# A recommendation tower on one core: unrolled h copied to PSUM, one split remainder made by GpSimd, and ten of layer 1's sixteen tiles split

## The reference, cut to what matters

```python
e = jnp.stack([tbl_0[ids[:, 0]], ..., tbl_31[ids[:, 31]]], axis=1)     # x: 1024 x 32 fields x 32
def _cin(x, Ws, bs):
    h = x
    for i, (W, b) in enumerate(zip(Ws, bs)):                            # O = 128, 128, 1
        z = jnp.einsum('bhd,bmd,ohm->bod', h, x, W.reshape(O, H, F))
        z = jax.nn.relu(z + b[None, :, None])
        if i < n_layers - 1:
            h, direct = (z[:, :half, :], z[:, half:, :])                # 64 rows go on, 64 are summed
        ...
    return jnp.sum(jnp.concatenate(directs, axis=1), axis=-1)
z = _cin(e, (W0, W1, W2), (b0, b1, b2))
h = relu(concat([z, dense_ctx]) @ W_top1 + b_top1); h = relu(h @ W_top2 + b_top2); y = h @ W_top3
```

## Time and profile before

| | us |
|---|---|
| time, median of 3 runs | 1158.95 (1157.48 to 1160.01) |
| span of the profiled execution | 1162.5 |
| busy: PE / DVE / ACT / POOL | 1116.8 / 1083.0 / 458.8 / 520.5 |
| first matmul | 28.4 |

### The profile page before, as it was taken

How to read it: one execution, slowest core, us unless ns; L and a number is a source line. 1 busy time by engine, 2 the same in 40 slices (tenths; PEclk the granted TensorE clock), 3 DMA queues, 4 the chain that set the end, 5 groups by cost and what they waited for, 6 DMA issues and landing times.

```text
span 1162.5 us, 10957 instructions
## 1 busy us (share of the span) xinstructions
PE 1116.8 (96%) x3608; PEld 652.8 (56%) x3608; DVE 1083.0 (93%) x604; ACT 458.8 (39%) x383; POOL 520.5 (45%) x270
## 2 busy tenths in 40 slices
PE   0699999999999999999999999999999999999998
PEld 0355555556555555556555565555555555555554
DVE  1599999999999999999999999999999999999963
ACT  0134444333444433344444334444333444443424
POOL 6702445654445555454456544455555544450000
PEclk9899999999999999999999999999999999999999
DMA  7654543466554435555543455454445545433200
GB/s 222 200 165 129 148 136 118 108 153 162 161 139 137 126 108 143 161 161 139 132 135 106 140 161 161 139 146 128 112 129 160 161 140 160 131 123 96 55 1 0
DMA packets 63413, 154.94 MB, mean 133 GB/s; under 512 B 12753, under 2 KB 29394, under 8 KB 63394
## 3 DMA queue, kind: packets, MB, share of 16 engines
q1 hardware_dynamic: 52562, 146.98, 42.5%
q0 software_dynamic: 8192, 4.21, 3.0%
q10 hardware_dynamic: 2640, 3.50, 1.0%
HBM read 95.79 MB, written 8.39 MB: 90 GB/s over the span
## 4 chain that ended last, share of the span: by engine, by line
PE 93%; issue 2%; DVE 2%; ACTq 1%; another core or an unknown queue 1%; ACT 1%; DMA 0%; SPq 0%; DVEq 0%
PE z_ps L543 89%; PE u_ps L543 2%; PE mlp_ps L543 1%; DVE raw L450 1%; DVE prod_lo L457 1%; DVE prod L411 1%; DMA h_roll<-h_roll 0%; SPq L328 0%; ACT prod_hi L760 0%; SPq L329 0%; ACT h_roll L729 0%; ACT direct L747 0%; ACTq L713 0%; ACTq L715 0%
## 5 line engine op out<-in xcount | busy, mean ns | idle before, releaser
L543 PE MATMUL z_ps<-prod,w_sb 128*128 128x512 f32 x1536 | 692.8, 597 | 39.2 <-issue 28.4
L303 POOL DMA_INDIRECT gathered<-in_table,rows_sb x256 | 504.9, 1972 | 499.5 <-DVE h2x L464 428.8
L543 PEld LDWEIGHTS z_ps<-prod,w_sb 128*128 128x128 f32 x1536 | 292.7, 191 | 350.6 <-issue 333.8
L760 ACT CAST prod_hi<-raw 128x2048 fp32r<-128x2048 f32 x128 | 243.9, 1905 | 396.5 <-DVE raw L450 389.4
L450 DVE TENSOR_TENSOR raw<-h_roll,x_roll 128x2048 f32<-128x2048 f32 x128 | 293.1, 2290 | 5.6 <-DMA h_roll<-h_roll 2.1
L457 DVE TENSOR_TENSOR prod_lo<-raw,prod_hi 128x2048 fp32r<-128x2048 f32 x128 | 292.0, 2281 | 2.6 <-ACT prod_hi L760 2.6
L411 DVE TENSOR_TENSOR prod<-h_roll,x_roll 128x2048 f32<-128x2048 f32 x128 | 292.6, 2286 | 0.0
L543 PE MATMUL z_ps<-prod_hi,w_hi 128*128 128x512 f32 x520 | 215.4, 494 | 0.4 <-DVE prod_lo L457 0.4
L543 PE MATMUL z_ps<-prod_lo,w_hi 128*128 128x512 f32 x520 | 164.1, 395 | 0.0
L543 PE MATMUL z_ps<-prod_hi,w_lo 128*128 128x512 f32 x520 | 163.8, 395 | 0.0
L411 DVE TENSOR_TENSOR prod<-x_base,x_roll 128x2048 f32<-128x2048 f32 x63 | 143.4, 2286 | 12.8 <-DMA x_roll<-x_dram 10.8
(11 more groups left out here) (56 smaller groups left out, 240.8 us busy)
## 6 DMA issues: line engine op xcount, KB each, us to landing
x_roll<-x_dram SPq DMA_DIRECT2D x128, 512.0 KB
x_base<-x_dram SPq DMA_DIRECT2D x32, 512.0 KB
h_roll<-h_roll SPq DMA_DIRECT2D x32, 448.0 KB, 4.6
h_roll<-h_roll SPq DMA_DIRECT2D x32, 384.0 KB, 5.4
h_roll<-h_roll SPq DMA_DIRECT2D x32, 320.0 KB
x_dram<-gathered SPq DMA_DIRECT2D x64, 128.0 KB
h_roll<-h_roll SPq DMA_DIRECT2D x32, 192.0 KB
gathered<-in_table,rows_sb POOLq DMA_INDIRECT x256
```

What stands on the lines that cost most here:

```text
L303: nc.gpsimd.indirect_dma_start(gathered[:, u, g * DIM:(g + 1) * DIM], None, table, bass.IndirectOffsetOnAxis(ap=rows_sb[:, col:col + 1], a ...
L543: return nc.tensor.matmul(*args, **kw)
L760: nc.scalar.copy(prod_hi[:, b % SPLIT_RING, :, :], raw[:, :, :]).then_inc(hi_ready, 1)
```

## The change

Layer 1's sixteen tiles are shared out anew: three whole pairs and five split pairs. The whole pairs are (a=1; x 0, 1), (a=0; x 0, 1) and (a=0; x 2, 3); the split pairs are B0 to B3 (a = 2, 3 by x 0, 1, 2, 3) and A1 (a=1; x 2, 3).

- ScalarE copies the unrolled h (a=0) into the PSUM tile `mlp_ps`, which only the last network used (`copy_h0`, one copy of 128 x 1024 a chunk). The two whole pairs with it read h from PSUM and x from SBUF.
- The remainder of B1 is made by GpSimd (`lo1`), the other four by VectorE.
- The gathers are issued a chunk at a time, three chunks ahead, each after the `lo1` of its step; before, they went out in groups of four chunks.
- Buffers: `prod` has two pairs (three before), `raw` two (one), `prod_hi` and `prod_lo` three (two), `x_base` one (two), and `top_b` is `x_base`, zeroed in the last chunk by GpSimd.
- The loads of `x_roll` 0 and 1 wait for the first two whole products of layer 1 two chunks before, 2 and 3 for B2 and B3; `x_part16` is loaded between.
- `sum_direct` and `layer2` come after the two products from PSUM.

```diff
-PAIRS1 = ROLLS
-RING = 3
-SPLIT_RING = 2
+WHOLE1 = 3
+B0, B1, A1, B2, B3 = range(5)
+SPLIT1 = 5
+RING = 2
+SPLIT_SLOT = (0, 1, 2, 0, 1)
+SPLIT_RING = 3
+RAW_SLOT = (0, 1, 0, 1, 0)
...
+            def lo1(c):
+                rounded = settled(pool, c * SPLIT1 + B1 + 1)
+                behind = settled(pool, lo_count(c, B0))
+                pool.wait_ge(hi_ready, rounded)
+                pool.wait_ge(lo_ready, behind)
+                nc.gpsimd.tensor_tensor(prod_lo[:, SPLIT_SLOT[B1], :, :], raw[:, RAW_SLOT[B1], :, :],
+                                        prod_hi[:, SPLIT_SLOT[B1], :, :], ALU.subtract).then_inc(lo1_ready, 1)
...
+                    base_free = settled(sp, first0(c - 1) + PAIRS0)
+                    free = [(prod_ready, settled(sp, first1(c - 2) + 2))] * 2 + [
+                        (raw_ready, settled(sp, (c - 2) * SPLIT1 + r + 1)) for r in (B2, B3)]
...
+                if isinstance(c, int) and c == 1:
+                    sp.wait_ge(prod_ready, PAIRS0)
+                    load_base(c)
...
-                for b in range(ROLLS):
-                    whole(first1(c) + b, slot1(c) + b, h_roll[:, s, 0:PAIR, :], twice(x_roll[:, s, b, :]))
+                split_product(c, u, B0)
+                if not is_last(c):
+                    split_rest16(c + 1)
+                if not is_first(c):
+                    rolled_once()
+                split_product(c, u, B1)
+                split_rest(c, B0)
+                dve.wait_ge(h0_copied, c + 1)
+                for k in range(PAIRS0):
+                    whole(first1(c) + 1 + k, slot1(c, u) + 1 + k, twice(mlp_ps[:, :]),
+                          x_roll[:, s, k * PAIR:(k + 1) * PAIR, :])
+                if not_first(c):
+                    layer2(c - 1, *before)
+                    sum_direct(c - 1, *before)
+                split_product(c, u, A1)
+                split_product(c, u, B2)
+                split_rest(c, A1)
+                split_product(c, u, B3)
+                split_rest(c, B2)
...
+                layer1(c, u, 0)
+                if not is_last(c):
+                    layer0_pairs16(c + 1)
+                if not_first(c):
+                    layer2_u(c - 1, (u - 1) % UNROLL)
+                split(z1_ps, c, B0)
+                layer1(c, u, 1)
+                split(z1_ps, c, B1)
+                layer1(c, u, 2)
+                split(z1_ps, c, A1)
+                split(z1_ps, c, B2)
...
+            def copy_h0(c, u):
+                act.wait_ge(h1_ready, 2 * (c + 1))
+                if not_first(c):
+                    act.wait_ge(prod_ready, first1(c - 1) + WHOLE1)
+                nc.scalar.copy(mlp_ps[:, :], h_roll[:, u % 2, 0, :]).then_inc(h0_copied, 1)
```

More of the change, by code:

```diff
@@ L96, in y_partition, with pool_makes_lo3, lo_count @@
     return FIELDS * j
-assert (PAIRS0 + PAIRS1) % RING == 0 and PAIRS1 % SPLIT_RING == 0
+def pool_makes_lo3(c):
+    return False
+def lo_count(c, r):
+    if not isinstance(c, int):
+        return c * LO_PER_CHUNK + LO_ORDER[r]
+    return sum(LO_PER_CHUNK + (0 if pool_makes_lo3(k) else LO_EXTRA) for k in range(c)) + LO_ORDER[r]
+assert UNROLL % RING == 0
 def build_tower(nc, gather_ids, row_base, table, w0, w0_swapped, w1_whole, w1_split, w2, b0, b1, b2,
@@ L282, in _, with make_rows @@
             pool.wait_ge(ids_loaded, 32)
-            def gather_group(group):
+            def make_rows(group):
                 cols = UNROLL * GATHERS
-                made = settled(pool, group + 1)
-                freed = [0 if isinstance(group, int) else settled(pool, (group - 1) * UNROLL + u + 1)
-                         for u in range(UNROLL)]
                 for u in range(UNROLL):
@@ L293, in gather_group, with gather @@
                                         ALU.add).then_inc(rows_made, 1)
+            def gather(c, u, group):
+                made = settled(pool, group + 1)
+                freed = settled(pool, c - UNROLL + 1)
                 pool.wait_ge(ids_loaded, 32)
                 pool.wait_ge(rows_made, made)
[L297 to L306, removed]
@@ L308, in _ @@
-            gather_group(0)
-            with pool.Fori(1, CHUNKS // UNROLL) as group:
-                gather_group(group)
+                wait(pool, h2x_ready, freed)
+                for g in range(GATHERS):
+                    col = u * GATHERS + g
+                    nc.gpsimd.indirect_dma_start(
+                        gathered[:, u, g * DIM:(g + 1) * DIM], None, table,
+                        bass.IndirectOffsetOnAxis(ap=rows_sb[:, col:col + 1], axis=0),
+                    ).then_inc(gather_done[u], 16)
@@ L312, in _ @@
+            make_rows(0)
+            for c in range(UNROLL - 1):
+                gather(c, c, 0)
+            over_chunks(pool, step)
         @block.sync
@@ L427, in products0 @@
                         dve.wait_ge(x_roll_loaded[s][b], (c - s + 2) * 8)
-                    whole(first0(c) + k, slot0(c) + k, twice(x_base[:, s, :]), x_roll[:, s, k * PAIR:(k + 1) * PAIR, :])
+                    whole(first0(c) + k, slot0(c, u) + k, twice(x_base[:, :]), x_roll[:, s, k * PAIR:(k + 1) * PAIR, :])
                 dve.wait_ge(gather_done[u], (group + 1) * (16 * GATHERS))
@@ new lines, in rolled_once @@
+                def rolled_once():
+                    dve.wait_ge(h1_ready, 2 * (c + 1))
+                    dve.wait_ge(h1_rolled[s][0], (c - s + 2) * 16)
+                    whole(first1(c), slot1(c, u), twice(h_roll[:, s, 1, :]), x_roll[:, s, 0:PAIR, :])
+                if is_first(c):
+                    rolled_once()
[3 more added lines that the diff above has]
+                if not is_first(c):
+                    rolled_once()
@@ L865, in lay_out @@
     w1 = a["L0_rec_W1"].reshape(P, HID, FIELDS)
[L866 removed]
+    whole = [(1, 0), (1, 1), (0, 0), (0, 1), (0, 2), (0, 3)]
+    split = [(2, 0), (3, 0), (2, 1), (3, 1), (1, 2), (1, 3), (2, 2), (3, 2), (2, 3), (3, 3)]
+    for name, tiles in (("w1_whole", whole), ("w1_split", split)):
         arrays[name] = np.stack([w1[:, (r + H_ROLL * k) % HID, (i + x_shift(quad, b)) % FIELDS].T
[L868 removed]
+                                 for k, b in tiles], axis=1)
     w2 = a["L0_rec_W2"].reshape(HID, FIELDS)
```

219 lines of the change are left out of this document (121 added, 98 removed).

## The result

The change made the kernel slower: 1166.81 us, median of five runs (1165.20 to 1170.21), beside 1160.01 for the kernel before on the same chip (1157.48 to 1161.79). The ratio is 1.0062 with a 95% interval of 1.0046 to 1.0077, so the loss of 0.6% is small but clear of the noise. The forecast was 1140.

A forecast was written before the change was run, and what follows sets the result against it. TensorE was taken as the bound at 33.80 us a chunk, VectorE only 0.37 faster. Gains of 17.7 over 30 chunks, 1.3 at the start and 0.6 at the end made 19.6: 1158.95 to 1139.4, called 1140 for scatter; range 1134 to 1157.

The forecast's parts named there:

- what covers GpSimd's remainder: Layer 1: GpSimd's estimated 4.6 us run from 8.2 to 12.8, hidden beside VectorE's PSUM products, 1.2 us to spare before A1.
- the ring of two: VectorE in layer 1: earliest held at the last whole product, at 10.1 us after TensorE's start on layer 0.
- 1.0 us later: Layer 1's first whole pair needs `relu1` by 6.7, gets it at 5.6; VectorE may run up to 1.0 us late.
- Rival C: VectorE and TensorE wait in turn through ScalarE, losing 0.5 to 0.6 us a chunk: 1157 to 1161; no-change chance 0.05.
- TensorE's need: TensorE per chunk: one split pair replaces a whole one, -0.63 us, from 33.80 to 33.17.
- products from PSUM at no extra cost: VectorE's layer 1 products reading h from PSUM: assumed to cost no more than from SBUF, nothing taken.
- rival B: PSUM products are held by GpSimd too, 4.0 us more a chunk: 1287, or 1213; chance 0.13, shared with long GpSimd overrun.
- VectorE's list: VectorE per chunk: fourteen large instructions still, two fewer waits of 0.11, so from 33.43 to 33.21 us.
- Rival A: GpSimd's subtraction overruns its window, costing from 5.8 us: 1150 at 6.1, over 1159 beyond 6.4; small-loss chance 0.14, shared.
- The start: First chunks: TensorE's start on chunk 2 counts as 85.0 against 86.29, a gain of 1.3 us.
- The bridge: Span to median: median taken as 3.55 us below the span, so span 1142.9 gives 1139.4.
- 0.6 at the end: Last chunk, bound by TensorE again: a gain of 0.6 us.

The follow-up runs named there:

- Experiments 1: Kernel after the change, with ScalarE's `relu1` ahead of B0's rounding instead of behind it: 1146.83 us, ratio 0.9890 to the kernel before.
- experiment 2: Kernel after the change, with VectorE's first whole product with h moved behind B1's product: 1143.64 us, ratio 0.9871 to the kernel before.
- 4: Kernel after the change, with ScalarE's copy of h to PSUM moved between B0's rounding and `relu1`: 1187.96 us, ratio 1.0256 to the kernel before.
- experiment 5: Kernel of experiment 2, with ScalarE's copy of h also moved between B0's rounding and `relu1`: 1156.82 us, ratio 0.9973 to the kernel before.
- experiment 6: Kernel of experiment 2, with the two products from PSUM reading h from SBUF again, copy still made: 1236.64 us, ratio 1.0669 to the kernel before.
- experiment 8: The kernel before the change, unchanged, profiled a second time: one run of 1158.27 us, span 1156.5 us.
- experiment 3: Kernel after the change, with both `relu1` ahead of B0's rounding and the first h product behind B1's: 1144.24 us, ratio 0.9867 to the kernel before.

## Why the prediction was wrong

*The step that failed* is under what covers GpSimd's remainder: "VectorE is held back earliest by the ring of two: the last whole product waits for TensorE's use of the first, at 6.7 + 3.43 = 10.1". With two buffers every whole product waits for the one two places ahead. The first product with h, which the working put at 1.4 us after TensorE's start of the step without a bound, waits for the use of layer 0's first pair, and that ends 3.6 us after TensorE's start on the chunk's layer 0 (625.60 to the held product's start at 629.24). So VectorE is held back two products earlier than the prediction said, and the "1.0 us later" that VectorE was allowed for `relu1` was not enough: 1.4 + 1.0 is 2.4, and the ring holds the product to 3.6. The 1.2 us between them are what the trace shows, as VectorE's wait of 1.23 in one chunk and TensorE's of 1.13 in another. Ring and `relu1` ask for two things that don't go together at 33.2 us a chunk, and the kernel alternates between them. Experiments 1 and 2 show each link, 4 the length.

*Rival C* had the right kind of mechanism and the wrong circle. Its sum, "1.95 + 2.52 + 3.43 + 0.3 + 24.1 = 32.3, under 33.21", closed over the held product at 10.2 within one chunk. The circle that decides goes on through TensorE's next layer 0 and closes only after two chunks, at 68.0. Searching for circles within one chunk couldn't find it. The circle that C did sum is real and its sum was good: with 1.1 us more, 33.4, it decides experiment 5, at 33.47. Even C's worst case, the whole gain lost, was too mild: a loop may be longer than the old bound, and this one was, by 0.20 a chunk.

*Right, and measured as such with the loop open (experiment 2):* TensorE's need, 33.17 against 33.20; GpSimd's remainder, 4.6 against 4.59 and inside its window; products from PSUM at no extra cost, so rival B falls; gathers and loads hidden. VectorE's list, 33.21, measured 33.08 in the kernel after, where nothing held it. The Trainium skill's 4497 ns for a float32 tensor_tensor of 2048 elements on GpSimd (GPSIMD Engine Reference, section 3.1) agrees to 0.11 us with the subtraction here (4607 ns). Rival A's condition, two SBUF inputs on both sides, is borne out by experiment 6, but its mechanism never came up, since the window held.

*The start* was mis-sized. "TensorE's start counts as 80.1 + 4.9 = 85.0 against 86.29", a gain of 1.3. Experiment 2's chunk 2 starts at 84.02, the kernel after's at 81.69. But the 86.29 was that of a late execution; in experiment 8 the same start is at 81.98. So the kernel after has 0.3 us of gain, experiment 2 a loss of 2.0. The edit of experiment 2 doesn't touch that stretch, so the 2.3 between the two are scatter. Half is the load of `x_base` (VectorE's product starts at 42.90 and at 44.09). The other half is TensorE's clock: it had stood some 8 us before layer 0 of chunk 1, and its granted clock up to the held product was 0.68 in the one (45.3 to 50.8 us) and 0.57 in the other (46.5 to 53.2).

*The bridge* from span to median ("3.55 below the span") took an execution's accident for a rule: the kernel before has a span of 1156.5 against 1158.27 on the second look.

With these put right the sum for experiment 2 is (135.22 - 132.78)/4 x 30 = 18.3, less 2.0 at the start, plus the forecast's 0.6 at the end: 16.9 us. Measured are 15.3 between the spans (1156.5 and 1141.2), and 15 of the time by the ratio of 0.9871. The end is borne out (57.28 us from TensorE's last wait for `relu1`, against 57.92). Of the 1.6 that are missing 1.24 are a wait of TensorE for VectorE at 92.28. The forecast's 19.6 would have been some 4 us too high even without the loop.

The version of experiment 2 is the best of the kernels here, 1143.64 us, 23 below the change as made; experiment 3, at 1144.24, can't be told from it.

## What to carry to other kernels

When a ring of buffers gets shorter, write down for every one of its users, not only the last, which use frees its buffer, and follow the waits until they close, over two iterations as well as over one (here the loop over one chunk stood some 0.7 us below the lists, and the one over two above them): the period is at least a loop's length divided by the iterations it spans, whatever the busy shares say. If the chain of waits changes engine from one iteration to the next, or two engines wait in turn, look for such a loop. The cheap repair is to move one instruction at one of its links, which took one exchange of neighbours here. A loop that hid behind a longer list can come out when the lists get shorter or a ring loses a buffer, so the loops have to be added up together with the lists.

## What the runs showed of the hardware

- While GpSimd's 128x2048 subtraction runs, VectorE's products with one input in PSUM keep 2.28 us (2282 ns over 64, kernel after), and GpSimd needs 4.54 to 4.63 us (4.57 to 4.60 in experiment 2). With both inputs in SBUF (experiment 6) GpSimd waited through two products in a row, 8.68 us in all, and the next one of VectorE stood 2.9 us.
- In experiment 4 TensorE stood 2.4 us in each fourth chunk. In three of the periods its granted clock then fell to 0.50, and a pair took 5.39 us in place of 3.69; in the period before these and the one behind them a wait of 2.4 us left it at 1.00.
- The kernel before, run twice, had spans of 1162.5 and 1156.5 us with the same period of 135.22. Of the difference 4.3 us arose at the start, with a ScalarE that stood 9.14 us in one of them, and 1.7 in the last chunk, where TensorE's granted clock fell in the same one.
